# A per-sample feed-forward: merged weights in plain fp32 from four 32-row tiles, read in place 32 floats apart

## The reference, cut to what matters

```python
gh = relu(einsum('bsd,hd->bsh', x, gfc1_w) + gfc1_b)
g  = (einsum('bsh,eh->bse', gh, gfc2_w) + gfc2_b).mean(axis=1)      # 32 samples x 8
W1m = W1 + einsum('be,efd->bfd', g, tv_W1)                          # 32 x 512 x 128
b1m = b1 + g @ tv_b1
W2m = W2 + einsum('be,edf->bdf', g, tv_W2)                          # 32 x 128 x 512
b2m = b2 + g @ tv_b2
h   = relu(einsum('bsd,bfd->bsf', x, W1m) + b1m[:, None, :])
out = einsum('bsf,bdf->bsd', h, W2m) + b2m[:, None, :]
# then x + out, a layer norm, and the residual
```

## Time and profile before

| | |
|---|---|
| median of three executions | 888.86 us |
| the profiled execution, its own time | 878.77 us |
| its span (first to last instruction) | 876.9 us |
| TensorE clock granted over the span, mean | 0.912 of full |
| PE / PEld busy | 703.5 us / 601.6 us |
| DVE / ACT / POOL busy | 583.2 us / 471.4 us / 359.0 us |
| the gate's tail, from 173 | 4 us |
| the merge, 177 to 233 | 56 us |
| the feed-forward, 233 to 298 | 65 us |

### The profile page before, as it was taken

One profiled execution on the slowest core, in us unless ns is written; L12 is line 12 of the kernel. 1 busy time (PEld: TensorE's weight loads), 2 busy tenths in 40 slices (PEclk: granted clock), 3 DMA queues, 4 the chain that ended last, 5 costly groups with the idle time before them and its releaser, 6 DMA issues.

```text
span 876.9 us, 18625 instructions
## 1 busy us (share of the span) xinstructions
PE 703.5 (80%) x5467; PEld 601.6 (69%) x5467; DVE 583.2 (67%) x1562; ACT 471.4 (54%) x1280; POOL 359.0 (41%) x593
## 2 busy tenths in 40 slices
PE   3888999999999957999989888755669768778720
PEld 2447998588899724888877776545669667667610
DVE  4946776689755495488898777664747556566524
ACT  5446555856656547677776665224336445444410
POOL 0220110078533242222254694797420545455551
PEclk9979999989999979699999999868779999999965
DMA  8100000023000399940000000001133656665537
GB/s 228 25 28 1 0 0 1 0 69 90 31 1 0 109 340 352 339 126 2 2 3 8 31 27 14 26 25 46 33 107 123 218 177 216 213 210 201 181 113 257
DMA packets 63418, 87.02 MB, mean 99 GB/s; under 512 B 8609, under 2 KB 48318, under 8 KB 63103
## 3 DMA queue, kind: packets, MB, share of 16 engines
q1 hardware_dynamic: 53791, 73.39, 25.7%
q0 software_dynamic: 5344, 10.80, 3.7%
q10 hardware_dynamic: 4224, 2.10, 0.8%
HBM read 24.70 MB, written 37.19 MB: 71 GB/s over the span
## 4 chain that ended last, share of the span: by engine, by line
PE 49%; DVE 17%; issue 13%; ACT 10%; another core or an unknown queue 3%; POOL 3%; DMA 2%; DVEq 1%; SPq 1%; POOLq 0%; ACTq 0%
PE ps3a L1121 3%; PE ps3a L1119 2%; PE ps L1051 2%; PE ps3b L1091 2%; DVE h_f L1889 2%; PE ps L986 2%; PE ps3a L986 2%; PE ps3b L996 2%; PE ps3a L1120 2%; PE ps3a L996 2%; DVE hT L668 2%; PE ps3a L1078 2%; DVE arena L1773 2%; PE ps3b L915 1%
## 5 line engine op out<-in xcount | busy, mean ns | idle before, releaser
L818 POOL DMA_INDIRECT rows_by_token<-yrow,homei x93 | 91.5, 984 | 113.2 <-DVE yrow L1907 89.8
L1375 ACT CAST h_hi<-h_f 128x384 fp32r<-128x384 f32 x86 | 44.1, 513 | 92.0 <-DVE h_f L1889 66.9
L700 POOL TENSOR_TENSOR mg_low<-tvc,mg_high 128x256 fp32r<-128x256 f32 x64 | 46.2, 743 | 40.7 <-DVE mg_high L1520 40.7
L1324 ACT ACTIVATE arena<-ps3a,arena 128x141 f32<-128x141 f32 x192 | 55.9, 389 | 11.7 <-DVE arena L1773 10.0
L1912 DVE TENSOR_TENSOR h_lo<-h_f,h_hi 128x384 fp32r<-128x384 f32 x86 | 48.1, 559 | 17.6 <-ACT h_hi L1375 8.8
L1889 DVE TENSOR_TENSOR h_f<-ps,h_s 128x384 f32<-128x384 f32 x43 | 23.9, 557 | 49.6 <-PE ps3a L1121 22.1
L1749 DVE RECIPROCAL arena<-ps 128x141 f32<-128x141 f32 x32 | 33.3, 1041 | 29.6 <-PE ps L1054 18.6
L1773 DVE TENSOR_REDUCE arena<-ps3a 128x2 f32<-128x282 f32 x96 | 38.7, 442 | 10.8 <-PE ps3a L1078 9.6
L1306 ACT ACTIVATE arena<-ps,vec,cst 128x141 f32<-128x141 f32 x32 | 15.1, 471 | 55.7 <-PE ps L1069 41.5
L1119 PE MATMUL ps<-x_hi,wb 128*128 128x384 f32 x62 | 23.4, 377 | 24.1 <-DVE x_lo L1874 20.6
L693 POOL COPY arena<-xn 128x141 f32 (+1 forms) x32 | 9.9, 310 | 78.0 <-PE ps3b L931 61.9
(11 more groups left out here) (422 smaller groups left out, 2666.0 us busy)
## 6 DMA issues: line engine op xcount, KB each, us to landing
rows_by_expert<-zeros SPq DMA_DIRECT2D x1, 18915.0 KB, 61.1
wb<-wparts SPq DMA_DIRECT2D x31, 512.0 KB
wb<-wparts SPq DMA_DIRECT2D x31, 256.0 KB
xrow<-rows_by_expert SPq DMA_DIRECT2D x31, 195.0 KB
rows_by_token<-zeros SPq DMA_DIRECT2D x2, 2304.0 KB, 44.3
tvc<-in_L_ffn_tv_W_dram SPq DMA_DIRECT2D x32, 128.0 KB
ysum<-rows_by_token SPq DMA_DIRECT2D x10, 320.0 KB, 6.2
arena<-in_x_dram SPq DMA_DIRECT2D x2, 1024.0 KB, 7.2
```

What stands on the lines that cost most here:

```text
L700: pool.tensor_tensor(mg_low[:, s, :], tvc[:, r, s * 256:(s + 1) * 256], mg_high[:, s, :].bitcast(F32), ALU.subtract).then_inc(S("mg_low"), 1)
L818: pool.indirect_dma_start(yt[:, :], bass.IndirectOffsetOnAxis(ap=homei[:, q, s:s + 1], axis=0), yrow[:, q, s, :], None, oob_is_err=True).t ...
L1324: ins = act.activation(b_e[:, q, h, :], bank[2 + i][:, (h % 2) * N:(h % 2) * N + N], ACT.Exp, bias=b_nm[:, q, h:h + 1])
L1375: act.copy(h_hi[:, s, 0:n], h_f[:, s, 0:n]).then_inc(S("h_hi"), 1)
```

## The change

1. **Loads.** `tvc` now holds four slices of 512 columns, each as four tiles of 32 partitions (eight tasks by four row groups j; the tile is the quarter i of 32 consecutive rows' groups). The base matrix goes to a buffer of its own, `wbase`, four partitions per tile. A slice is eight DMAs, four of 32 partitions and four of 4 partitions; 16 slices are 128 DMAs. The first four slices are loaded early, with constant addresses; the twelve others each wait for `mg_mm`, the end of the matmuls on the slice four before it. The two memsets that zeroed unused partitions go.
2. **Merge.** No `mg_high`, no `mg_low`, no `gb_high`, no `gb_low`. PE takes fp32 directly: for each 128-column block c of a slice, four matmuls of 32 rows (one for each tile i, each with a bank of its own), then four of 4 rows that add the base matrix through `gone`, a block of ones and zeros. That is 32 fp32 matmuls with a 128-column moving operand for each slice. ACT copies banks i = 0, 1 and DVE banks i = 2, 3, once per slice; a semaphore counts slices rather than pieces.
3. **Layout.** In `w1m` and `w2m` the sample is now the innermost index: a copy writes runs of 32 neighbouring floats, and one sample's weights lie 32 floats (128 bytes) apart.
4. **Feed-forward.** PE's stationary operand is `merged_for(0, t)` or `merged_for(1, t - 1)`: the sample's weights in place, 128 columns at a step of 32 floats. The copies into `wst` by ACT (L1287) and POOL (L707) go, with their semaphores `f_w1` and `f_w2`. PE's loop is written out over the 33 steps. The biases move to a buffer `bmb`, and the gate's hidden values to unused space in the arena.

The core of the diff:

```diff
-                    for half in range(2):
-                        if not (is_known(n) and n == 0):
-                            sp.wait_ge(S("mg_low"), n * 8 + (4 * r + 2 * half - 6))
-                        sp.dma_start(tvc[0:64, r, cols], tvr[:, bass.ds(at, 512)]).then_inc(S(f"tv_in{r}{half}"), 16)
-                        sp.dma_start(tvc[64:72, r, cols], bsr[:, bass.ds(at, 512)]).then_inc(S(f"tv_in{r}{half}"), 16)
+                if not (is_known(n) and n == 0):
+                    sp.wait_ge(S("mg_mm"), n * 4 + (r - 3))
+                for i in range(4):
+                    sp.dma_start(tvc[32 * i:32 * i + 32, r], tv[i, :, bass.ds(at, 512)]).then_inc(S(f"tv_in{r}"), 16)
+                    sp.dma_start(wbase[32 * i:32 * i + 4, r], base[i, :, bass.ds(at, 512)]).then_inc(S(f"tv_in{r}"), 16)
...
             def merge(n, r):
-                    for k in range(2):
-                        dst, at = bank[4 * r + s][:, k * 256:(k + 1) * 256], slice(k * P, (k + 1) * P)
-                        pe.matmul(dst, mg_high[:, s, at], gb_high[:, :], start=True, stop=False, skip_group_check=True)
-                        pe.matmul(dst, mg_high[:, s, at], gb_low[:, :], start=False, stop=False, skip_group_check=True)
-                        mm = pe.matmul(dst, mg_low[:, s, at], gb_high[:, :], start=False, stop=True, skip_group_check=True)
+                for c in range(4):
+                    at = slice(c * P, (c + 1) * P)
+                    for i in range(4):
+                        pe.matmul(bank[4 * (r % 2) + i][:, at], tvc[32 * i:32 * i + 32, r, at], gblk[32 * i:32 * i + 32, :],
+                                  start=True, stop=False, skip_group_check=True)
+                    for i in range(4):
+                        mm = pe.matmul(bank[4 * (r % 2) + i][:, at], wbase[32 * i:32 * i + 4, r, at], gone[32 * i:32 * i + 4, :],
+                                       start=False, stop=True, skip_group_check=True)
+        def merged_for(w, b):
+            m = w1m.rearrange("p j i n b -> p (j i n) b") if w == 0 else w2m.rearrange("p k j i n b -> p (k j i n) b")
+            return m[:, :, bass.ds(b, 1)].rearrange("p f b -> p (f b)")
...
             def ffn_step(t, r):
                     for k in range(4):
-                        mm = pe.matmul(bank[2 * r + k // 2][:, (k % 2) * N:(k % 2) * N + N], wst[:, r, k * P:(k + 1) * P],
+                        mm = pe.matmul(bank[2 * r + k // 2][:, (k % 2) * N:(k % 2) * N + N], merged_for(0, t)[:, k * P:(k + 1) * P],
                                        sample(xn, t), start=True, stop=True, skip_group_check=True)
...
-            run_steps(pe, B, 1, ffn_step, 4)
+            for t in range(B + 1):
+                ffn_step(t, t % 2)
...
-                    act.copy(wst[:, r, 0:F], w1m[:, bass.ds(t, 1), 0:F].rearrange("p a f -> p (a f)")).then_inc(S("f_w1"), 1)
-                pool.tensor_copy(wst[:, r, F:2 * F], w2m[:, bass.ds(t, 1), :].rearrange("p a f -> p (a f)")).then_inc(S("f_w2"), 1)
```

More of the change, by code:

```diff
@@ L283, in early_fusion @@
         used[0] = 0
[L284 to L287 removed]
+        w1m = take(F * B).rearrange("p (j i n b) -> p j i n b", j=4, i=4, b=B)
+        ghid = arena[:, F * B:F * B + 8 * N].rearrange("p (k a n) -> p k a n", k=4, a=2)
+        w2m = take(F * B).rearrange("p (k j i n b) -> p k j i n b", k=4, j=4, i=4, b=B)
+        tvc = sb("tvc", [P, 4, 512], scope=early)
         tvb = sb("tvb", [E + 1, F + D], scope=early)
         g9 = sb("g9", [E + 1, B + 1], scope=early)
[L290 to L291 removed]
+        gblk = sb("gblk", [P, 4 * B], scope=early)
+        gone = sb("gone", [P, 4 * B], scope=early)
+        bmb = sb("bmb", [P, B, 5], scope=early)
+        gcol = sb("gcol", [P, B], scope=early)
         ghm = sb("ghm", [P, B], scope=early)
+        wst = sb("wst", [P, 2, 2 * F], scope=early)
         merging = ctx.enter_context(ExitStack())
[L295 to L298, removed]
+        wbase = sb("wbase", [P, 4, 512], scope=merging)
         merging.close()
[L300 removed]
         hbuf = sb("hbuf", [P, 2, 4, N], scope=early)
@@ L950, in _ @@
             pe.wait_ge(S("g9_ready"), 2)
-            pe.matmul(bank[5][0:72, 0:B], C("rep", E + 1), g9[:, 0:B], start=True, stop=True).then_inc(S("grep_mm"), 1)
+            pe.matmul(bank[5][:, 0:B], C("rep", E + 1), g9[:, 0:B], start=True, stop=True).then_inc(S("grep_mm"), 1)
             pe.wait_ge(S("tvb_in"), 64)
@@ L971, in _ @@
             pe.wait_ge(S("bm_copied"), 1)
-            for r in range(2):
+            for r in range(4):
                 merge(0, r)
-            with pe.Fori(1, 8) as n:
-                for r in range(2):
+            with pe.Fori(1, 4) as n:
+                for r in range(4):
                     merge(n, r)
-            pe.wait_ge(S("mg_act"), 32)
-            pe.wait_ge(S("mg_dve"), 32)
+            pe.wait_ge(S("mg_act"), 16)
+            pe.wait_ge(S("mg_dve"), 16)
             def ffn_step(t, r):
@@ L1528, in merge @@
-            def merge(w, n, last=False):
-                for r in range(2):
-                    following = (n, 1) if r == 0 else (n + 1, 0)
-                    for s in range(4):
-                        if not (last and r == 1):
-                            high(*following, s)
-                        if s % 2 == 1:
-                            take(w, n, r, s)
-            for s in range(4):
-                high(0, 0, s)
-            for w in range(2):
-                with dve.Fori(4 * w, 4 * w + 4 - w) as n:
-                    merge(w, n)
@@ new lines, in _ @@
+            for w in range(2):
+                with dve.Fori(2 * w, 2 * w + 2) as n:
+                    for r in range(4):
+                        dve.wait_ge(S("mg_mm"), n * 4 + (r + 1))
+                        for i in range(2, 4):
+                            ins = dve.tensor_copy(merged_dst(w, n * 4 + (r - 8 * w), i),
+                                                  bank[4 * (r % 2) + i].rearrange("p (c j b) -> p c j b", c=4, j=4))
+                        ins.then_inc(S("mg_dve"), 1)
@@ L1546, in ffn_step @@
+            dve.wait_ge(S("mg_act"), 16)
+            dve.wait_ge(S("mg_dve"), 16)
             def ffn_step(t, r):
```

122 lines of the change are left out of this document (43 added, 79 removed).

## The result

The changed kernel takes 933.88 us (median of 4 runs, 928.63 to 938.04) against 889.12 us (4 runs, 888.16 to 889.52) for the kernel before: ratio 1.053, 95% interval 1.049 to 1.057. Its profiled execution took 933.74 us, with a span of 931.5. The medians differ by 44.8 us, the two profiled executions by 55.0; I come back to that gap in the last experiment.

What follows compares the result with a forecast made beforehand. The merge was taken as a ring of three engines, DVE fullest, and the feed-forward as PE alone. 878.77 + 3.9 (merge) + 48.0 (feed-forward) gave 930.7, put at 940 on the median's scale; range 886 to 955.

Steps and rivals of the forecast that it cites:

- The feed-forward, +48.0: Feed-forward: PE's weight loads at a step of 32 floats take 0.218 us, 512 of them 111.9 us, less 63.84.
- The factor of 1.9: Feed-forward: stepped DVE and ACT writes cost 1.84 and 2.0 times contiguous ones, so PE's 0.115 us load was multiplied by 1.9.
- 5 ns to spare: Feed-forward before the change: the 0.115 us weight load is hidden behind the 0.120 us matmul with 5 ns to spare.
- The merge, +3.9: Merge: the feed-forward would begin at 237.7 instead of 233.76, +3.9 us, with bounds from -6.5 to +7.4.
- SP's issuing is what is late next: Merge: SP's loads at 1.08 us a pair, 4.3 us a slice, 51.8 us for twelve, exceed PE's 1.9 or 3.8.
- the lower bound of 0.88: Merge: a pair of SP's loads takes 0.88 us if the 4-row DMA costs what a one-row DMA does.
- the forecast's 237.7: End of the merge: last DMA landed at 233.4, then 2.8 us of PE and 1.5 of copies and semaphores.
- Smaller things: PE's written-out loop and the memsets before the first attention, put at nothing.
- The 10.1 us between profile and median: Whole kernel before: median 888.86 against profiled 878.77 us, 10.1 us added at the end of the sum.
- B: Rival in the feed-forward: the strided load stays hidden and only the merge's term is left, 892.8 us; chance 0.25.
- D: Rival in the feed-forward: PE's clock falls to half, +59.0, 951.8 us; a 0.251 us load, 957, belongs here too; chance 0.10.
- C: Rival in SP's loop: pairs at 0.88 us, strided load hidden, feed-forward 6.5 us early, 882.4 us; chance 0.12.

Runs made afterwards that it cites:

- the last experiment: The changed kernel and the kernel before, both unaltered, measured again on one chip: 858.07 us against 809.63, ratio 1.060.
- The ladder: The changed kernel with each group of four samples reading its feed-forward weights at another step, from 1 to 33 floats; 915.37 us.
- the pairs: The changed kernel with merged weights in pairs of samples, two floats side by side; 809.54 us in one run against 808.64 for the kernel before.
- the kernel with rows of zeros: The changed kernel with each sample's weights contiguous and base matmuls over 32 rows, 28 of them zeros; 801.76 us against 808.64 before, ratio 0.991.

## Why the prediction was right

*The feed-forward, +48.0.* Right: +49.1 measured, 0.220 us an instruction where the forecast had 0.218. The read with a step cost about as much more as the stepped writes do: 0.220 us is 1.9 times the load's 0.115, beside their 1.84 and 2.0. That the memory is the reason which all share no run shows. The factor of 1.9 is no constant, and that it came within 2 ns is in part luck: the same factor stands against 0.234 and 0.240 us at steps of 4 and 8 floats. The ladder and the pairs show where it holds: from a step of four floats on (0.219 to 0.240 us), and not at two (0.121 us for PE, 686 ns for DVE's copy in runs of two). With the step at 2 floats the same argument would have promised 48 us as well, and the true term would have been zero. The "5 ns to spare" fit: step 3, at 0.174, was already exposed, and step 2 was not.

*The merge, +3.9.* The start of the feed-forward moved by -0.2 us, inside the bounds, but the step that led there failed: "SP's issuing is what is late next". PE never waited for a load. The 48 pairs took 0.88 us each, waits included, not 1.08, because the issue of 4 rows takes 0.26 to 0.31 us and of 32 rows 0.32, where I had priced them by the 64-row and 8-row issues of the old loop; the lower bound of 0.88 from the earlier trace rows was the right row. Against that the forecast had PE's slice at 1.9 us at full clock and 3.8 at half, and left open which of the two would hold; only the last slice's figure entered the sum. It stayed at half for all sixteen, 3.44 us a slice.

What each error was worth can be read from the kernel with rows of zeros, where SP issues its last load at the same time, 222.81, and PE has the full clock: its feed-forward starts at 228.8, 8.9 us before the forecast's 237.7. PE at half clock put the changed kernel's start back by 4.8, to 233.56. Two errors of opposite sign nearly met, which is luck. The forecast's own terms had the second bound: 16 x 3.8 = 61 us of PE from 176 end the merge at 237, as late as SP did, and it should have been named beside it.

*Smaller things.* Copies at 0.69 and 0.59 us (forecast 0.675 and 0.634), written-out loop and reading in place at nothing: right. The 10.1 us between profile and median, added at the end, is not a property of the change and did not belong to the changed kernel: its profile lies at its median. The forecast against the profile alone, 930.7, was 3 us from the 933.74 measured.

*Rivals.* B fell with the first row of the feed-forward. D's clock did not fall (0.97 and 1.00); its load of 0.251 us is above every step of the ladder. C was right on SP's pair, at 0.88 us, and wrong on the load.

## What to carry to other kernels

Before a tile is laid out for its writer, look at the step at which its reader reads it and at the length of the runs that its writer writes. Here two floats at a place cost DVE's copies nothing (686 ns, as with 32) and ACT's less than a tenth (639 against 589), and a step of two floats cost TensorE's loads behind matmuls of 141 columns nothing (0.121 against 0.120 us). Single floats made the reads or writes 1.7 to 2 times as long: 1169 ns on DVE and 1188 on ACT at a step of 512 floats, 0.220 us on TensorE at 32. A layout in pairs can serve a reader and a writer that want opposite orders. When tiles of few rows replace full ones, read the granted clock of the new stretch before trusting its instruction count (0.50 here with groups of 4 rows, 0.96 with the same groups over 32), and try the same instructions over all rows of the tile. Work out every engine's time for a slice at both clocks before naming the late one: here TensorE was the bound at a clock of 0.50, with 3.44 us a slice, and harmless at 1.00, where four tiles in 0.11 us make 1.8 us a slice, an estimate, beside SP's 3.5.

## What the runs showed of the hardware

- Matmuls on 32-row tiles, every second group of which read 4 rows, ran at a granted clock of 0.50 for 55 us though PE was never idle; the same stream with 32 rows, 28 of them zeros, rose to full clock early and had 0.96 over its merge. Without the second groups the clock rose too, between 180 and 183, and was 0.50 from 183.5 on, with PE busy for 26.9 of 38.5 us. What decides between rising, staying and falling is not settled by these runs.
- A weight load of 128x128 fp32 with its 141-column matmul takes 0.120 us at a step of 1 float, 0.121 at 2, 0.174 at 3, 0.234 at 4, 0.240 at 8, 0.219 at 16, 0.220 at 32, 0.231 at 33. Why 16 and 32 are cheaper than 4 and 8 is open.
- DVE copies 512 elements from PSUM with runs of 8 bytes in 686 ns, as with 128 bytes; with single floats 512 apart it takes 1.0 to 1.34 us.
- SP issues a DMA of 32 rows in 0.32 us and one of 4 rows in 0.26 to 0.31, whether a row has 2 or 4 KB.
- One and the same kernel took 809 to 889 us in the four groups of runs; of 67 us between two traces, 64 lay in the experts' stage, whose weights are streamed in.
